# VectorE's order in the first six steps of layer 0, and where TensorE transposes the words of tiles 3 and 4

## The chip, the cores and the metric
The kernel runs on one core of a Trainium2 chip. The metric is the device time of one execution in microseconds, the median of the runs made. Everything is set down against one profiled execution, whose own time is given below.

## The reference
Two graph attention layers over N = 8192 nodes with 256 features and a dense adjacency matrix of int32 that is nearly empty:

```python
# layer 0
h = relu(layernorm(x)); Wh = h @ W
e = (Wh @ a[:256])[:, None] + (Wh @ a[256:])[None, :]
e = where(adj == 0, -1e9, e)
x = x + leaky_relu(softmax(e, axis=1) @ Wh, 0.2)
# layer 1
h = relu(layernorm(x))
e = leaky_relu((h @ a[:256]) + (h @ a[256:]).T, 0.01)
e = where(adj > 0, e, -9e15)
x = x + softmax(e, axis=1) @ h
```

In layer 0 the row's own score cancels in the softmax, so a row of the result is a masked sum of weighted rows of `Wh`, divided by the masked sum of the weights.

## The kernel before
The rows are cut into T = 64 tiles of 128. A prologue normalises x, projects it (`transpose_h`, `project`) and makes `V0`, the weighted rows of `Wh` in two fp16 parts. Then layer 0 goes over the tiles, and layer 1 follows; the change lies in layer 0's first steps.

What happens to tile t of layer 0, engine by engine:

- **SyncE** (`whole`) loads the tile's 4 MB of adjacency in four quarters (`load`; a quarter waits for the conversion of the same quarter one tile earlier), and stores the packed words, the new x and the new h (`store_words`, `store_x1`, `store_h`), all in one queue in a written order.
- **ScalarE** (`step`) converts the quarters to fp8 (`convert`, tile t + 3 in step t), copies the transposed words from PSUM (`copy_words`, tile t + 1), scales the sums of tile t - 1 (`copy_sums`, which makes `ysb`), and takes the root and the relu of layer 1's layernorm for tile t - 1 (`roots1`, `finish`).
- **VectorE** (`step`) folds the fp8 masks into words in four parts (`fold`, tile t + 2; part 0 waits for the four conversions of that tile), finds the positions of the row's edges (`make_keys`, `extract`, and `decode`, whose long part `decode_bits` runs in steps 2, 6, 10 and so on, and whose short part `decode_list` runs in every step from 2), makes the reciprocal for tile t - 1 (`normalise`), adds x (`add_x`, which waits for `ysb`), and expands the copied words of tile t + 1 into the masks `adjT` in eight instructions (`unpack`, which waits for `copy_words`).
- **TensorE** runs `aggregate` for tile t: 128 matmuls (64 row blocks `jb`, two parts) of `adjT` and `V0` into a bank. It waits first for the masks of this tile (`adjT_ready`) and for `ysb` of tile t - 2, whose bank it overwrites. Behind the matmuls of `jb == turn_at` it puts `turn` of tile t + 1, four transposes of folded words, which wait for `fold` part 3 of that tile. The default of `turn_at` is 4. Tile 1 has it at 48; tiles from 2 on run in a loop, two tiles a round.

Two tiles' worth of `adjT`, banks and words alternate. Every engine works its instructions in program order; step t of VectorE and ScalarE begins when tile t - 1 is summed, and so stands beside TensorE's sums of tile t.

Of the kernel before, what the change touches and what calls it, by code (L numbers as in the profile page):

```python
# [30 lines left out]
def two_layer_graph_attention(nc, x, adj, w0, a0, a1, key_pos, ident, tri, caps, row_ids, out):  # L31
# [32 lines left out]
    T = N // P  # L64
# [17 lines left out]
    XB = 4  # L82
    LAG = 5
    XL = 1
    UN = 4
    VU = 16
    NPK = 4
# [3 lines left out]
    NS = T - SP0  # L91
    assert NS % UN == 0 and UN == NX == NPK
    KW = 16
# [10 lines left out]
    SORT = NS + 2  # L104
# [29 lines left out]
    with outer:  # L134
# [13 lines left out]
        with ctx:  # L148
            def sb(name, shape, dt):
                return ctx.enter_context(nc.sbuf_tensor(name, shape, dt))  # L150

            def sem(name):
# [43 lines left out]
            kraw = tail[:, 0:NK]  # L196
            khi = tail[:, NK:NK + UN * KT].rearrange("p (u s) -> p u s", u=UN)
            ki = tail[:, NK + UN * KT:NK + 2 * UN * KT].rearrange("p (u s) -> p u s", u=UN).bitcast(i32)
            ktop = sb("ktop", [P, UN, KT], f32)
            kb = sb("kb", [P, UN, KT], f32)  # L200
            kone = kraw.bitcast(f16)[:, 0:UN * ROUNDS * KT]\
                .rearrange("p (u s) -> p u s", u=UN)
# [107 lines left out]
            def offset(t):  # L310
                return SPARSE if t < NS else DENSE

            @block.sync
            def _(sp):
# [43 lines left out]
                def store_x1(t, off, b):  # L358
                    sp.wait_ge(x1_ready, t + 1)
                    sp.dma_start(x1_d[bass.ds(t + off, 1), :, :].rearrange("o p n -> p (o n)"),  # L360
                                 x1[:, b, :]).then_inc(x1_out[b], 16)
# [5 lines left out]
                def whole(t):  # L367
# [7 lines left out]
                    if LAG <= t:  # L375
                        store_x1(t - LAG, offset(t - LAG), (t - LAG) % NX)
                    if XL <= t < T + XL:
                        load_x(t - XL, offset(t - XL), (t - XL) % NX, t - XL < NX)
                    if LAG + 1 <= t:
# [3 lines left out]

                for t in range(T + XL):
                    whole(t)
                for i in range(3):
                    sp.wait_ge(scattered[i], 16 * len(range(i, NS, 3)))
                sp.dma_start(rec[:, :, :], rec_d.rearrange("(m p) c -> p m c", p=P)).then_inc(rec_in, 16)
                for t in range(T + XL, T + LAG):
                    whole(t)  # L390
# [183 lines left out]
            def _(dve):  # L574
# [109 lines left out]
                with dve.Fori(0, T // VU) as k:  # L684
                    for j in range(VU):
                        t = k * VU + j
# [5 lines left out]
                def normalise(t, b):  # L692

                    dve.wait_ge(acc_ready, t + 1)
                    nc.vector.reciprocal(rden[:, b:b + 1], acc[b][:, D:DV]).then_inc(rden_ready, 1)  # L695
# [140 lines left out]
                        decode_end(e)  # L836

                def step(t, j, n_in, x1_reuse, kept, off, ahead=True, folds=True, listed=False,
                         taken=False, e=None):

                    normalise(t - 1, (j - 1) % 2)
                    if folds:
                        fold(t + 2, j % 2, 0)
                    if taken:
                        extract(t + 1, (j + 1) % UN)
                    add_x(t - 1, (j - 1) % NX, n_in, x1_reuse, kept, off)
                    if ahead:
                        unpack(t + 1, (j + 1) % 2, (j + 1) % NPK)
                    if folds:
                        fold(t + 2, j % 2, 1)  # L850
                        fold(t + 2, j % 2, 2)
                    scale_h(t - 1)
                    if folds:
                        fold(t + 2, j % 2, 3)
                    if e is not None:
                        decode(e, (j + 2) % UN)
                    if listed:
                        make_keys(t + 2, j % 2)
                    dots(t - 1, (j - 1) % NX, kept)
# [62 lines left out]
                dve.wait_ge(hh_ones, 1)  # L922
                for t in range(1, T):
                    step(t, t % UN, *counts(t), ahead=t + 1 < T, folds=t + 2 < T, listed=t + 2 < NS,
                         taken=t + 1 < NS, e=(t - 2) // UN if 2 <= t < NS + 2 else None)
                    if t == SORT:
                        sort_totals()
                    if t == SORT + 1:
                        sort_scan()
                    if t == SORT + 2:  # L930
                        sort_ranks()
# [6 lines left out]
            @block.tensor  # L938
            def _(pe):
                pe.wait_ge(w_in, 16 * 3)  # L940
                pe.wait_ge(ucol_ready, 2)

                def transpose_h(t):
                    pe.wait_ge(h_ready, t + 1)
                    if t >= 2:
                        pe.wait_ge(hT_ready, t - 1)
                    for c in range(2):
                        last = nc.tensor.transpose(tps[t % 2][:, c * P:(c + 1) * P],
                                                   H[:, t, c * P:(c + 1) * P], idf[:, :])
                    last.then_inc(tr_ready, 1)  # L950

                def project(t):
                    pe.wait_ge(hT_ready, t + 1)
                    if t >= 3:
                        pe.wait_ge(wh_ready, t - 2)
                    for c in range(2):
                        last = nc.tensor.matmul(wps[t % 3][:, 0:DV], hT[:, t % 2, c, :], w_sb[:, c, :],  # L957
                                                start=(c == 0), stop=(c == 1))
                    last.then_inc(proj_ready, 1)

                def turn(t, b, reuse=True):

                    pe.wait_ge(fold_ready, t * 3 + 3)
                    if reuse:
                        pe.wait_ge(pk_ready, t - 1)
                    pe.sem_inc(words_due, 1)
                    words = fold1[:, b, 1, :].bitcast(bf16)
                    for q in range(BQ):
                        last = nc.tensor.transpose(turned[b].bitcast(bf16)[:, q * P:(q + 1) * P],  # L969
                                                   words[:, q * P:(q + 1) * P], idb[:, :])  # L970
                    last.then_inc(words_ps, 1)

                def aggregate(t, b, v0_wait=False, reuse=True, turn_at=T // 16):

                    pe.wait_ge(adjT_ready, t + 1)
                    if reuse:
                        pe.wait_ge(ysb_ready, t - 1)
                    pe.sem_inc(masks_due, 1)
                    for jb in range(T):
                        if v0_wait:  # L980
                            pe.wait_ge(v0_ready, jb + 1)
                        for s in range(2):
                            q, i, h = place(jb)
                            last = nc.tensor.matmul(acc[b][:, 0:DV], adjT_h[:, b, i, q, :, h],  # L984
                                                    V0[:, jb, s, 0:DV], start=(jb == 0 and s == 0),
                                                    stop=(jb == T - 1 and s == 1))
                        if jb == turn_at:
                            turn(t + 1, 1 - b)
                    last.then_inc(acc_ready, 1)

                for t in range(T):
                    transpose_h(t)
                    if t >= 1:
                        project(t - 1)
                    if t == T - 14:
                        pe.wait_ge(idb_ready, 1)
                        turn(0, 0, False)
                project(T - 1)
                turn(1, 1, False)
                pe.wait_ge(wh_ready, T)  # L1000
                pe.wait_ge(ones_set, 2)
                aggregate(0, 0, v0_wait=True, reuse=False, turn_at=None)
                aggregate(1, 1, reuse=False, turn_at=3 * T // 4)
                with pe.Fori(1, SORT // 2) as k:
                    for b in range(2):
                        aggregate(k * 2 + b, b)
                for b in range(2):
                    aggregate(SORT + b, b)
                pe.wait_ge(const_in, 16 * 5)
                pe.wait_ge(totals_ready, 1)  # L1010
                nc.tensor.matmul(kps[0][:, 0:KC], trib[:, 0:P], sums2[:, 1, :], start=True, stop=False)
                nc.tensor.matmul(kps[0][:, 0:KC], trib[:, P:2 * P], sums2[:, 0, :], start=False, stop=True)\
                    .then_inc(rank_ps, 1)
                with pe.Fori(SORT // 2 + 1, T // 2 - 1) as k:
                    for b in range(2):
                        aggregate(k * 2 + b, b)
                aggregate(T - 2, 0)
                aggregate(T - 1, 1, turn_at=None)
# [667 lines left out]
```

## Time and profile before

| | us |
|---|---|
| median of 3 runs | 1916.56 (1912.78 to 1921.1) |
| profiled execution, its own time | 1914.35 |
| its span on the core | 1912.5 |
| TensorE busy, of the span | 1691.5 |
| VectorE busy | 1203.0 |
| ScalarE busy | 973.4 |
| GpSimd busy | 651.6 |

The profile is one execution. Layer 0's sums run on TensorE from about 105 to about 1058 us, layer 1 from there to the end. An average over the whole span hides where an engine waits; it is read from the timeline of the stretch. In the rows further down, a line such as `[8.78 <-DVE adjT L658]` says that the engine sat idle for 8.78 us before the first instruction of the row, and that the instruction of line 658 on VectorE (DVE) ended the wait. L984 are the matmuls of layer 0, L969 the transposes of words, L627 to L641 the four parts of `fold`, L655 and L658 `unpack`, L695 `normalise`, L492 `copy_words`, L532 `copy_sums`, L519 `roots1`.

### The profile page before, as it was taken

What the parts mean: (1) busy time and instruction counts of PE and PEld (TensorE: products, weight loads), DVE (VectorE), ACT (ScalarE), POOL (GpSimd) and SP (SyncE); (2) the same over time, 40 slices, a digit from 0 to 9 for tenths busy, and PEclk for the clock granted to TensorE, in tenths of its full rate; (3) what the DMA queues carried; (4) which work ended last, traced back from release to release, by engine and by line L of the source; (5) the groups of instructions that cost most, each with busy time, mean ns of one, the idle gap of its engine ahead of it and who ended that gap; (6) DMA issues with size and microseconds to landing.
All of it is one profiled execution on the core that took longest, in us unless ns stands there. A gap on an engine that the chain in (4) does not pass through costs nothing. (4 is left out here: it accounts for less than half of the span.)

```text
span 1912.5 us, 37724 instructions
## 1 busy us (share of the span) xinstructions
PE 1691.5 (88%) x13955; PEld 1391.3 (73%) x13955; DVE 1203.0 (63%) x4595; ACT 973.4 (51%) x1367; POOL 651.6 (34%) x607
## 2 busy tenths in 40 slices
PE   6888999999999999999999397677888888978878
PEld 5646888888888888888888285454666667757657
DVE  7488888988888888674444377652435445435434
ACT  5987665665666556666662375432333233323322
POOL 0000000000000000026665548755656657665562
PEclk9998999999999999999999698877889889979889
DMA  8529998888988889989994534533333333433331
GB/s 287 182 76 386 342 349 325 314 311 321 354 320 326 318 310 331 355 333 378 386 379 104 130 94 134 160 80 88 101 89 83 111 89 94 117 100 99 88 92 52
DMA packets 142801, 410.60 MB, mean 215 GB/s; under 512 B 26193, under 2 KB 90066, under 8 KB 109906
## 3 DMA queue, kind: packets, MB, share of 16 engines
q1 hardware_dynamic: 108434, 329.85, 47.6%
q0 software_dynamic: 27904, 73.43, 13.9%
q10 hardware_dynamic: 6336, 5.77, 1.0%
q8 instruction: 62, 1.02, 0.2%
q14 instruction: 65, 0.53, 0.1%
HBM read 368.94 MB, written 40.03 MB: 214 GB/s over the span
## 5 line engine op out<-in xcount | busy, mean ns | idle before, releaser
L984 PE MATMUL banks<-HV,adjT 128*128 128x257 f16 x8192 | 938.8, 274 | 16.7 <-DVE adjT L658 8.8
L984 PEld LDWEIGHTS banks<-HV,adjT 128*128 128x128 fp8e4 x8192 | 792.5, 98 | 148.2 <-DVE HV L688 23.7
L1639 PE MATMUL banks<-Vp,adjp 128*128 128x257 f16 x2560 | 540.6, 292 | 115.4 <-issue 59.2
L1639 PE MATMUL banks<-Vn,adjn 128*128 128x257 f16 x2560 | 538.1, 291 | 48.9 <-issue 47.7
L1264 POOL DMA_INDIRECT gat<-h_of_layer,rec x420 | 465.8, 1109 | 275.5 <-issue 117.9
L444 ACT ACTIVATE adj_f<-adj_i 128x2048 fp8e4<-128x2048 int32 x256 | 480.1, 1898 | 6.6 <-DMA adj_i<-in_adj 6.5
L1300 ACT ACTIVATE adjn<-h1bc,nh 128x512 fp8e5<-128x512 f32 x320 | 212.1, 716 | 446.2 <-remote 272.1
L1639 PEld LDWEIGHTS banks<-Vp,adjp 128*128 128x128 fp8e4 x2560 | 261.2, 103 | 192.3 <-issue 126.5
L1639 PEld LDWEIGHTS banks<-Vn,adjn 128*128 128x128 fp8e4 x2560 | 262.2, 103 | 124.8 <-issue 76.5
L425 POOL DMA_DIRECT2D HV<-x_after_layer x44 | 25.5, 580 | 773.4 <-DVE rank L911 741.3
L1473 DVE TENSOR_TENSOR adjn<-adjp,adjn 128x1024 uint16<-128x1024 uint16 x80 | 55.4, 692 | 334.8 <-ACT adjn L1300 296.0
L1534 DVE SCALAR_TENSOR_TENSOR sacc<-gat,w,sacc 128x257 f32<-128x257 f32 x332 | 152.5, 477 | 0.0
L492 ACT ACTIVATE pk<-banks 128x512 uint16<-128x512 uint16 x64 | 37.9, 593 | 170.3 <-PE banks L969 143.9
L695 DVE RECIPROCAL rden<-banks 128x1 f32<-128x1 f32 x64 | 10.7, 168 | 145.9 <-PE banks L984 115.3
L655 DVE TENSOR_SCALAR adjT<-pk 128x512 uint16<-128x512 uint16 x448 | 94.6, 282 | 0.0
L957 PE MATMUL banks<-w_sb,hT 128*128 128x257 f32 x256 | 68.9, 392 | 15.6 <-ACT hT L456 15.3
L627 DVE SCALAR_TENSOR_TENSOR fold<-adj_f 128x1024 int32<-128x1024 int32 x64 | 77.2, 1206 | 7.4 <-ACT adj_f L444 7.4
L418 POOL DMA_INDIRECT x_after_layer_sorted<-HV,rank x44 | 66.5, 1512 | 13.4 <-issue 12.2
L525 ACT ACTIVATE hh<-x,nmr,rstd 128x256 f32<-128x256 f32 x64 | 38.4, 601 | 53.6 <-DVE nmr L727 45.8
L1515 DVE TENSOR_TENSOR w<-e 128x5 f32<-128x5 f32 (+2 forms) x88 | 13.9, 157 | 77.8 <-ACT e L1321 58.5
L519 ACT ACTIVATE std<-mv,eps 128x1 f32<-128x1 f32 x64 | 18.8, 294 | 86.0 <-DVE mv L719 83.9
L1255 POOL DMA_INDIRECT out<-sout,rec x44 | 46.5, 1058 | 43.1 <-DVE sout L1550 31.8
(158 smaller groups left out, 1395.2 us busy)
## 6 DMA issues: line engine op xcount, KB each, us to landing
adj_i<-in_adj SPq DMA_DIRECT2D x256, 1024.0 KB
h_of_layer<-hh SPq DMA_DIRECT2D x64, 129.0 KB
hs<-h_of_layer SPq DMA_DIRECT2D x64, 129.0 KB
xt<-in_x SPq DMA_DIRECT2D x64, 128.0 KB
packed_adj<-pk SPq DMA_DIRECT2D x64, 128.0 KB
x_after_layer<-x SPq DMA_DIRECT2D x64, 128.0 KB
HV<-in_x SPq DMA_DIRECT2D x14, 512.0 KB, 8.8
gat<-h_of_layer,rec POOLq DMA_INDIRECT x420
```

The source lines that it names most:

```text
L418: pool.indirect_dma_start(x1s_d, bass.IndirectOffsetOnAxis(ap=rank[:, m:m + 1], axis=0), HV[:, T + m % SH, 0:D], None).then_inc(xs_out[m % ...
L444: nc.scalar.activation(adj_f[:, b, q * QC:(q + 1) * QC], adj_i[:, q, :], ACT.Copy, scale=2.0, saturate=False).then_inc(conv_done, 1)
L627: nc.vector.scalar_tensor_tensor(four, whole[:, 0:4 * GW], 1, whole[:, 4 * GW:8 * GW], ALU.logical_shift_right, ALU.bitwise_or)\
L655: last = nc.vector.tensor_scalar(adjT[:, b, i, :], pk[:, pb, :], PAIR << i, 6 - i, ALU.bitwise_and, ALU.logical_shift_left)
L957: last = nc.tensor.matmul(wps[t % 3][:, 0:DV], hT[:, t % 2, c, :], w_sb[:, c, :], start=(c == 0), stop=(c == 1))
L984: last = nc.tensor.matmul(acc[b][:, 0:DV], adjT_h[:, b, i, q, :, h], V0[:, jb, s, 0:DV], start=(jb == 0 and s == 0), stop=(jb == T - 1 and ...
L1255: pool.indirect_dma_start(out, bass.IndirectOffsetOnAxis(ap=rec[:, m, OWN:OWN + 1], axis=0), sout[:, m % NOUT, :], None).then_inc(so_out[m ...
L1264: pool.indirect_dma_start(gat[:, k % NBUF, s - s0, :], None, h_d, bass.IndirectOffsetOnAxis(ap=rec[:, m, s:s + 1], axis=0))\
L1300: i = nc.scalar.activation(adjn_b[:, c % 2, jb // 2, :, jb % 2], h1bc[:, g2, :], ACT.Relu, scale=-BIG, bias=nh2[:, tiles[j]:tiles[j] + 1], ...
L1473: nc.vector.tensor_tensor(part, both, part, ALU.bitwise_and).then_inc(neg_ready, 1)
L1534: nc.vector.scalar_tensor_tensor(acc, x, w, acc, ALU.mult, ALU.add)\
L1639: mm = nc.tensor.matmul(bank[2 * i + part][:, 0:DV], m[:, i * P:(i + 1) * P], V[:, j, s, 0:DV], start=(j == 0 and s == 0), stop=(j == T - ...
```

## The change
On VectorE, steps 1 to 6 (`hurry`, t < HURRY = 7) get another order: behind `normalise` come `unpack` of tile t + 1, then `extract` of tile t + 1, then part 0 of `fold` of tile t + 2, then `add_x`. Before, it was `fold` part 0, `extract`, `add_x`, `unpack`. The other instructions of the step keep their places, and steps from 7 on are as they were.

On TensorE, tiles 2 and 3 are taken out of the loop and written out. The transposes of tile 3's words stand behind row block 48 of tile 2's sums, those of tile 4's words behind row block 32 of tile 3's sums; before, both stood behind row block 4. The loop begins at tile 4. No instruction is added or removed on VectorE.

```diff
+    HURRY = 7
                 def step(t, j, n_in, x1_reuse, kept, off, ahead=True, folds=True, listed=False,
-                         taken=False, e=None):
+                         taken=False, e=None, hurry=False):
 
                     normalise(t - 1, (j - 1) % 2)
-                    if folds:
+                    if hurry:
+                        unpack(t + 1, (j + 1) % 2, (j + 1) % NPK)
+                        extract(t + 1, (j + 1) % UN)
                         fold(t + 2, j % 2, 0)
-                    if taken:
+                    elif folds:
+                        fold(t + 2, j % 2, 0)
+                    if taken and not hurry:
                         extract(t + 1, (j + 1) % UN)
                     add_x(t - 1, (j - 1) % NX, n_in, x1_reuse, kept, off)
-                    if ahead:
+                    if ahead and not hurry:
                         unpack(t + 1, (j + 1) % 2, (j + 1) % NPK)
                     if folds:
                         fold(t + 2, j % 2, 1)
...
-                         taken=t + 1 < NS, e=(t - 2) // UN if 2 <= t < NS + 2 else None)
+                         taken=t + 1 < NS, e=(t - 2) // UN if 2 <= t < NS + 2 else None, hurry=t < HURRY)
...
                 aggregate(0, 0, v0_wait=True, reuse=False, turn_at=None)
                 aggregate(1, 1, reuse=False, turn_at=3 * T // 4)
-                with pe.Fori(1, SORT // 2) as k:
+                aggregate(2, 0, turn_at=3 * T // 4)
+                aggregate(3, 1, turn_at=T // 2)
+                with pe.Fori(2, SORT // 2) as k:
                     for b in range(2):
                         aggregate(k * 2 + b, b)
```

## Rows read from the trace of the kernel before

**Rows 1.** Busy time by stretch: PE, PEld, DVE, ACT, POOL, clock, DMA share, GB/s.
```profile
100.00:150.00 50.00, 39.86 (x260) 21.28 (x260) 40.24 (x117) 42.54 (x75) 0.32 (x1) 0.93 0.33 126
...
300.00:400.00 100.00, 100.00 (x911) 87.39 (x910) 86.94 (x401) 65.31 (x59) 0.00 (x0) 1.00 0.92 334
...
900.00:1000.00 100.00, 100.00 (x911) 87.38 (x910) 47.12 (x181) 63.39 (x56) 67.64 (x62) 1.00 1.01 383
```

**Rows 2.** Timeline of TensorE, 95 to 175: start, length, engine, line, count, idle before.
```profile
105.32 5.17 PE L984 MATMUL banks<-HV,adjT 128*128 128x257 f16 x26 [6.02 <-DVE HV L688]
...
143.29 0.38 PE L969 MATMUL banks<-idb,fold 128*128 128x128 bf16 x4
143.51 3.51 PE L984 MATMUL banks<-HV,adjT 128*128 128x257 f16 x30
155.81 2.31 PE L984 MATMUL banks<-HV,adjT 128*128 128x257 f16 x10 [8.78 <-DVE adjT L658]
...
173.66 0.38 PE L969 MATMUL banks<-idb,fold 128*128 128x128 bf16 x4
```

**Rows 3.** Timeline of TensorE, 150 to 330.
```profile
188.18 0.38 PE L969 MATMUL banks<-idb,fold 128*128 128x128 bf16 x4
188.41 14.47 PE L984 MATMUL banks<-HV,adjT 128*128 128x257 f16 x128
...
246.29 0.38 PE L969 MATMUL banks<-idb,fold 128*128 128x128 bf16 x4
```

**Rows 4.** Timeline of VectorE, 95 to 250: steps 1 to 3.
```profile
148.77 1.22 DVE L627 SCALAR_TENSOR_TENSOR fold<-adj_f 128x1024 int32<-128x1024 int32 x1 [6.67 <-ACT adj_f L444]
...
153.89 1.47 DVE L655 TENSOR_SCALAR adjT<-pk 128x512 uint16<-128x512 uint16 x7
155.28 0.28 DVE L658 TENSOR_SCALAR adjT<-pk 128x512 uint16<-128x512 uint16 x1
...
160.04 1.23 DVE L627 SCALAR_TENSOR_TENSOR fold<-adj_f 128x1024 int32<-128x1024 int32 x1 [0.70 <-ACT adj_f L444]
...
165.35 1.47 DVE L655 TENSOR_SCALAR adjT<-pk 128x512 uint16<-128x512 uint16 x7
...
179.06 0.17 DVE L695 RECIPROCAL rden<-banks 128x1 f32<-128x1 f32 x1
179.14 1.21 DVE L627 SCALAR_TENSOR_TENSOR fold<-adj_f 128x1024 int32<-128x1024 int32 x1
...
184.43 1.47 DVE L655 TENSOR_SCALAR adjT<-pk 128x512 uint16<-128x512 uint16 x7
...
186.02 0.68 DVE L632 SCALAR_TENSOR_TENSOR fold<-fold 128x512 int32<-128x512 int32 x1
...
187.29 0.42 DVE L641 SCALAR_TENSOR_TENSOR fold<-fold 128x256 int32<-128x256 int32 x1
```

**Rows 5.** Timeline of ScalarE, 95 to 190 and 190 to 262.
```profile
143.71 0.60 ACT L492 ACTIVATE pk<-banks 128x512 uint16<-128x512 uint16 x1 [0.29 <-PE banks L969]
...
151.35 0.46 ACT L532 ACTIVATE ysb<-banks,rden 128x256 f32<-128x256 f32 x1
...
196.13 0.29 ACT L519 ACTIVATE std<-mv,eps 128x1 f32<-128x1 f32 x1 [1.88 <-DVE mv L719]
...
203.13 0.60 ACT L492 ACTIVATE pk<-banks 128x512 uint16<-128x512 uint16 x1
```

**Rows 6.** Busy time by stretch, columns as in rows 1, around the first gap.
```profile
148.00:152.00 4.00, 0.00 (x0) 0.00 (x0) 3.15 (x12) 3.01 (x3) 0.00 (x0) 0.77 1.03 421
152.00:156.00 4.00, 0.19 (x2) 0.16 (x3) 3.85 (x16) 3.57 (x4) 0.00 (x0) 0.50 1.02 430
...
160.00:162.00 2.00, 2.00 (x18) 1.64 (x16) 1.92 (x5) 1.78 (x2) 0.00 (x0) 0.89 1.00 399
```

**Rows 7.** Timeline of VectorE, 186 to 232 and 232 to 262: steps 6, 7.
```profile
216.39 0.17 DVE L695 RECIPROCAL rden<-banks 128x1 f32<-128x1 f32 x1 [2.12 <-PE banks L984]
...
235.47 0.17 DVE L695 RECIPROCAL rden<-banks 128x1 f32<-128x1 f32 x1
...
243.69 0.42 DVE L641 SCALAR_TENSOR_TENSOR fold<-fold 128x256 int32<-128x256 int32 x1
...
247.04 0.17 DVE L695 RECIPROCAL rden<-banks 128x1 f32<-128x1 f32 x1
```

## The prediction, made before the changed kernel had run
> **What bounds the kernel now.** I read the busy times by stretch first, to see which engine sets the pace of layer 0. From 300 to 400 us TensorE is busy for all 100 us, and from 900 to 1000 us again, while VectorE has 87 and 47 us of work in them [rows 1]. So from some early point TensorE runs without a gap until its sums end, and whatever moves that point moves everything behind it, one for one. From 100 to 150 us it is busy for 40 of 50 us: there the time can change.
>
> Next came TensorE's timeline, for the gaps. Between the sums of tile 1 (last 30 matmuls from 143.51 to 147.02) and those of tile 2 (from 155.81) it idles 8.78 us and is released by VectorE's masks, `adjT` [rows 2]. Behind it, the transposes of the words mark the tiles: they stand at 173.66 (tile 4), 188.18 (tile 5) and 246.29 (tile 9), and 246.29 minus 188.18 is four times 14.53, so a tile takes 14.53 us and nothing stalls after tile 2 [rows 2, 3].
>
> Then VectorE's timeline, for why the masks were late. It sits idle for 6.67 us until 148.77, for the conversions that `fold` of tile 3 needs, then extracts, adds x of tile 0, and unpacks tile 2 only from 153.89 to 155.56 [rows 4]. The words of tile 2 had been copied by 144.31 [rows 5]. The reader is to see two things: the masks could have been made in that idle time; and from 148.77 on VectorE itself has hardly a gap for three steps (step 2 has its fold at 160.04 and is over by 179.06, the unpacking of tile 4 runs from 184.43 to 186.1, and the fold of tile 5 ends at 187.71) [rows 4]. TensorE began tile 4 at 188.18 less 1.13 us for ten matmuls, 187.05, and asked for the fold of tile 5 at 188.18 [rows 3]. VectorE was ready only 1.0 and 0.5 us ahead. In these steps a delay of VectorE is soon one of TensorE.
>
> **The change, part by part.** The sum goes against the profiled execution, 1914.35 us (span 1912.5); the median of the runs is 1916.56.
>
> Step 1, order on VectorE. Unpacking tile 2 starts at 144.35 and takes 1.67 us, so it ends at 146.0. TensorE is free at 147.02, but it also waits for `ysb` of tile 0, for the bank that tile 2's sums overwrite. ScalarE makes that from 151.35 to 151.81, behind conversions that wait for their data [rows 5]; nothing in the change touches those. With the 0.25 us that lay between the last mask and the first matmul [rows 2, 4], tile 2 starts at 152.06: 3.75 us earlier. The wait has changed its owner and lost less than half. The extraction fits into the rest of the idle time; `fold` of tile 3 still starts at 148.77; x is added from 151.85 instead of 152.42. The fold's last part, behind the square root, ends near 156.8 against 157.2, and the step's dots stay where they were, behind the same conversions. So step 2 begins at 159.2 as before.
>
> The clock. At 148 to 152 us the granted share is 0.77, at 152 to 156 it is 0.50, the lower of the two levels (1.2 GHz), and at 160 to 162 it is 0.89 [rows 6]. TensorE had been idle since 147.02. A share of 0.77 in four microseconds means that the fall was near 150.2, before my 152.06. So tile 2 starts slow again: before, it took from 155.81 to 173.66 less 1.13, that is 172.53, or 16.72 us instead of 14.53 [rows 2, 3]. The price is 2.19 us, and I keep it. Tile 2 ends at 168.78.
>
> The later transpose of tile 3. It stands behind matmul pair 48 of 63, with 30 matmuls left (3.40 us) and 0.22 us of its own, so it starts at 165.16 and ends at 165.54; the copy on ScalarE is done at 166.18. The old place, pair 4, would have come near 154 us, ahead of the fold at 156.8, and cost TensorE 2.5 us or more; this is saved. But now VectorE's step 2 begins with a wait for these words: from 159.2 to 166.18 it does nothing, and extraction, fold, x, decoding and dots queue behind it. On ScalarE the conversions stand behind `copy_words` of tile 3 as well, and on SyncE the loads behind `store_words`; I price that at 0, since the queues move 0.92 of their time in the steady part and TensorE waits for none of it there [rows 1]; if this cover fails, it is the slower rival below. Unpacking tile 3 ends at 167.85, in time for 168.78. Tile 3's sums then run to 183.31. Tile 4's transpose, at pair 32, comes at 176.3, and its fold is there at 174.8: no stall.
>
> Step 2, the rest. From the fold to the unpacking was 165.35 minus 160.04, 5.31 us; the unpacking took 1.59 until the next instruction (184.43 to 186.02), which puts its end in step 2 at 166.94, and from there to 179.06 was 12.12 us, the first long decoding among it [rows 4]. New: 166.18 + 1.59 + 5.31 + 12.12 = 185.20, 6.1 us later than before. Now unpacking tile 4 comes first, from 185.28 to 186.95, and TensorE starts tile 4 at 187.20. Before it was 187.05. The 3.75 us are gone, and TensorE has idled 3.9 us ahead of tile 4.
>
> Step 3. TensorE wants the fold of tile 5 after ten matmuls. That fold stands behind extraction, fold and x (5.29 us, 179.14 to 184.43) and 1.69 us more (to the end of 187.29's, from 186.02) [rows 4]: 186.87 + 5.29 + 1.69 = 193.85, and 0.2 for the semaphore gives 194.05. Before: 188.18. That is 5.87 us later. TensorE idles about 5 us here, and after it the clock is taken as low, for 2.19 us once more; 0 if the ten matmuls and the shorter gaps keep it up. The running loss is 8.06 us.
>
> On the clock, the Trainium skill ("TensorE: Matmul & The Clock Gate", What's actually happening) has the lower level as the default, released by activity and lost when idle. The trace agrees in the gap before tile 2 [rows 6]; by the rule both new gaps lead to the low level, which is the 2.19 us already counted.
>
> Steps 4 to 6. Here unpacking moves ahead of its words: the transpose comes ten matmuls into the sums, and ScalarE's copy comes after its conversions. From the root to the copy's end ScalarE took 203.13 + 0.60 minus 196.13, 7.6 us, of which 0.75 were a wait that goes [rows 5]: 6.85. With x of tile 2 at 192.1, words 5 come at 199.1. From one set of words to the next, while VectorE waits for them, are then 1.59 + 5.25 + 0.1 + 6.85, 13.8 us. A step with a list decoded is 11.57 us (235.47 to 247.04) [rows 7], so step 5 starts at 199.1 + 11.57 = 210.7 and words 6 come at 212.9; step 6 starts at 224.5 and words 7 come at 226.7. Step 6 holds the long decoding: 235.47 minus 216.39 is 19.08 [rows 7], so step 7 starts at 245.8. There, in the old order, masks 8 are done at 252.8 (5.39 + 1.67) and the fold of tile 9 at 245.8 + 8.64 = 254.4 [rows 7]. TensorE, 8.06 late, ends tile 7 at 253.2 and asks for that fold at 254.36; it gets it at 254.6. Against 246.29 this is 8.3 us. If the clock cost nothing in step 3, TensorE would arrive 2.2 us earlier here and wait for the same VectorE instructions: 8.3 again. After step 7 the order is the old one, VectorE catches up by step 9, and nothing is recovered, as TensorE has no gap to give back.
>
> The two sums taken out of TensorE's loop: tile 1's sums are written out as well and ran at 3.51 us for 30 matmuls, the loop's at 14.47 for 128 [rows 2, 3], 0.117 and 0.113 us each. I take 0; from the difference it could be 1 us for 256, and on the other side nothing speaks for a gain.
>
> The sum: -3.75 from the first gap, +3.90 given back in step 2, +5.72 in step 3 (5.87 less the 0.15 already counted), +2.19 clock, +0.24 at tile 9: 8.3 us. Forecast 1916.56 + 8.3 = 1924.9 (1922.7 for a profiled execution). Bounds: no clock price, with steps 4 to 6 quick enough to leave no wait at tile 9, gives +5.9; another low-clock start at tile 9 and 1 us of straight code give +11.5.
>
> **The rivals.**
> Gain kept: the masks' wait is shorter and later steps absorb the delay. The time is then 1916.56 - 3.75 = 1912.8. For it: the gap is real and the early masks remove their part. Against: VectorE had 1.0 and 0.5 us in hand and is set back 6.1. Chance 12%.
>
> Small loss: VectorE's rows in steps 2 and 3 shrink, because the fold and the extraction no longer wait for anything, and half of the 5.87 goes: about +3, 1919.6. Against: the rows show no waits in them. Chance 10%.
>
> Slower beyond the forecast: step 6, where words 7 arrive and the 19.08 us step starts. Each microsecond by which they are later than 226.7 comes back as a wait for masks 8 and fold 9; from 1.3 us on the total passes +9.6, and with 2 us and a low clock behind it, it is 8.3 + 2 + 2.19 = 12.5, 1929.1. For it: ScalarE's copy stands behind four conversions whose data must have landed, on a DMA that I took to have room. Chance 16%.
>
> **How the numbers follow.** Forecast 62%, own range 1921 to 1929. The bound of 0.5%, about what a measurement of this kernel can tell from no change, is 9.6 us. The forecast lies 1.3 us under it, and runs of one kernel spread by some 4 us either way, so a third of it falls beyond: 21% slower, 41% same. The small loss is same (10%), the slower rival slower (15 and 1), the kept gain same 8, faster 4. Together slower 0.36, same 0.60, faster 0.04. The range, 1915 to 1931, leaves out the kept gain and the worst of the slower rival.
>
> **What would show it.** Right: TensorE's first gap ends at 152, released by ScalarE's `ysb`; VectorE idles about 7 us before unpacking tile 3; gaps on TensorE of about 4 us before tile 4, released by `adjT`, and of about 5 us ten matmuls later, released by `fold`; waits of VectorE for ScalarE's words in steps 4 to 6. Wrong: masks 4 done before 183.3, or tile 5's transposes before 189; then the gain stands. Wrong too if TensorE shows gaps inside the written-out sums.

## The result and the profile after

| | us |
|---|---|
| the changed kernel, first measurement | 1947.42 (1935.75 to 1950.49, 5 runs) |
| the kernel before beside it | 1917.0 (1912.78 to 1928.01, 5 runs) |
| ratio | 1.0137, 95% interval 1.0092 to 1.0183 |
| profiled execution of the changed kernel | 1935.75, span 1933.7 |
| changed kernel again, 12 runs against 29 | 1760.79 against 1754.18, ratio 1.0032 (1.0015 to 1.0049) |
| changed kernel a third time, 12 runs against 23 | 1918.05 against 1913.08, ratio 1.0038 (1.0003 to 1.0073) |

The change makes the kernel slower: all three intervals lie above 1. The forecast was +8.3 us, in a range up to 1931, and the first median lay 16 us above the range. The two later measurements give 0.0032 x 1754 = 5.6 us (2.6 to 8.6 by the interval) and 0.0038 x 1913 = 7.3 us (0.6 to 14). All ratios here and below are those on record, taken from undisturbed runs alone, and need not equal the quotient of two medians of all runs. The text takes the two parts in turn: layer 0, which the prediction worked out and the traces confirm, and layer 1, which the change does not touch and whose time moved by 11.9 us between the first two traces.

TensorE's timeline of the changed kernel, to be read beside [rows 2, 3]. The matmuls of layer 0 are now L989, the transposes of words L974:

```profile
144.12 0.38 PE L974 MATMUL banks<-idb,fold 128*128 128x128 bf16 x4
144.34 3.52 PE L989 MATMUL banks<-HV,adjT 128*128 128x257 f16 x30
152.86 13.71 PE L989 MATMUL banks<-HV,adjT 128*128 128x257 f16 x98 [5.00 <-issue]
166.42 0.38 PE L974 MATMUL banks<-idb,fold 128*128 128x128 bf16 x4
...
177.37 0.38 PE L974 MATMUL banks<-idb,fold 128*128 128x128 bf16 x4
177.59 7.09 PE L989 MATMUL banks<-HV,adjT 128*128 128x257 f16 x62
188.51 1.85 PE L989 MATMUL banks<-HV,adjT 128*128 128x257 f16 x10 [3.83 <-DVE adjT L659]
195.29 0.58 PE L974 MATMUL banks<-idb,fold 128*128 128x128 bf16 x4 [4.92 <-DVE fold L642]
195.67 16.21 PE L989 MATMUL banks<-HV,adjT 128*128 128x257 f16 x128
211.72 0.38 PE L974 MATMUL banks<-idb,fold 128*128 128x128 bf16 x4
...
255.62 0.38 PE L974 MATMUL banks<-idb,fold 128*128 128x128 bf16 x4 [0.16 <-DVE fold L642]
```

The wait of 5.00 us is put down to "issue" here; what came last is seen on ScalarE, where `ysb` is done at 152.77, and TensorE starts at 152.86:

```profile
152.31 0.46 ACT L533 ACTIVATE ysb<-banks,rden 128x256 f32<-128x256 f32 x1
```

The words of tile 2 are turned (transposed) at 144.12 here and at 143.29 before; this 0.83 us comes from the prologue, and is taken off every time below that is compared. The one gap of 8.78 us has become three: 5.00, 3.83 and 4.92. The last transposes shown, those of tile 9, stand at 254.79 against 246.29: 8.5 us late, where 8.3 was forecast. The sums end as late:

```profile
1031.00 27.66 PE L984 MATMUL banks<-HV,adjT 128*128 128x257 f16 x246
```
```profile
1040.32 27.66 PE L989 MATMUL banks<-HV,adjT 128*128 128x257 f16 x246
```

The first row is of the kernel before (the sums end at 1058.66), the second of the changed one (1067.98, or 1067.15 without the prologue's part). So layer 0 is 8.5 us longer. Layer 1 took 1912.5 - 1058.66 = 853.8 us before and 1933.7 - 1067.98 = 865.7 after: 11.9 of the 21.2 us between the two spans lie where no instruction was changed. The medians are 30.4 us apart; the other 9 us lie between the profiled executions and the medians, and no trace shows in which layer.

VectorE's timeline of the changed kernel shows who made TensorE wait, to be read beside [rows 4]:

```profile
145.17 1.51 DVE L656 TENSOR_SCALAR adjT<-pk 128x512 uint16<-128x512 uint16 x7 [2.25 <-ACT pk L493]
...
152.79 0.43 DVE L707 SCALAR_TENSOR_TENSOR lr<-ysb 128x256 f32<-128x256 f32 x1 [1.96 <-ACT ysb L533]
...
167.47 1.50 DVE L656 TENSOR_SCALAR adjT<-pk 128x512 uint16<-128x512 uint16 x7 [7.14 <-ACT pk L493]
...
186.49 0.17 DVE L696 RECIPROCAL rden<-banks 128x1 f32<-128x1 f32 x1
186.58 1.48 DVE L656 TENSOR_SCALAR adjT<-pk 128x512 uint16<-128x512 uint16 x7
...
194.72 0.42 DVE L642 SCALAR_TENSOR_TENSOR fold<-fold 128x256 int32<-128x256 int32 x1
```

The masks of tile 2 are made from 145.17, while VectorE would have been idle. But the masks of tile 3 wait 7.14 us for their words, and all the work behind them, the decoding of step 2 among it, moves. The masks of tile 4 start at 186.58, and TensorE has stood idle for them since 184.68. The fold of tile 5 ends at 195.14 and TensorE turns its words at 195.29.

Busy time by stretch, columns as in [rows 1], for the clock, beside [rows 6]:

```profile
152.00:156.00 4.00, 3.14 (x15) 2.25 (x16) 2.33 (x6) 3.36 (x4) 0.00 (x0) 0.50 1.04 435
...
183.00:188.00 5.00, 1.68 (x16) 1.22 (x13) 4.72 (x27) 1.31 (x2) 0.00 (x0) 1.00 0.76 252
188.00:190.00 2.00, 1.49 (x10) 1.12 (x10) 1.91 (x12) 0.97 (x1) 0.00 (x0) 0.76 0.06 16
190.00:192.00 2.00, 0.36 (x2) 0.00 (x0) 1.96 (x5) 0.00 (x0) 0.00 (x0) 0.50 0.94 311
192.00:196.00 4.00, 0.71 (x6) 0.67 (x7) 3.65 (x19) 2.40 (x3) 0.00 (x0) 0.50 0.58 199
```

Tile 2 starts at the lower level (0.50, 1.2 GHz), as forecast. In the gap ahead of tile 4 the clock is still full and falls only once the sums have begun again (0.76 from 188 to 190, where they begin at 188.51); it stays low through the third gap and into the sums behind it, and is full again from 200 us on.

### The profile page after: what moved, and what is told of

Its sections match the earlier page's. It is cut to its first block and busy times, and to the rows that moved or that the text cites. A ratio compares the mean times of both kernels' runs of the same rounds, so it can differ in the third digit from the quotient of the medians.

```text
span 1933.7 us, 37717 instructions
## 1 busy us (share of the span) xinstructions
PE 1691.4 (87%) x13955; PEld 1390.9 (72%) x13955; DVE 1204.3 (62%) x4595; ACT 972.2 (50%) x1367; POOL 648.6 (34%) x607
## 5 line engine op out<-in xcount | busy, mean ns | idle before, releaser
L989 PE MATMUL banks<-HV,adjT 128*128 128x257 f16 x8192 | 941.9, 274 | 16.7 <-DVE HV L689 7.5
L989 PEld LDWEIGHTS banks<-HV,adjT 128*128 128x128 fp8e4 x8192 | 794.1, 98 | 149.7 <-DVE HV L689 23.3
L1328 ACT ACTIVATE e<-gat,hb 128x5 f32<-128x5 f32 (+3 forms) x176 | 41.5, 288 | 40.0 <-DMA gat<-h_of_layer,rec 40.0
```

What stands on the lines that cost most here:

```text
L1328: nc.scalar.activation(e8[:, k % 2, i, 0:s1 - s0], gat[:, k % NBUF, 0:s1 - s0, DV], ACT.Exp, scale=scale, bias=hb[:, i, m:m + 1]).then_inc ...
```

## The experiments

In what follows a theory is named by the letter that it has in the expectations. Layer 0 of each run is compared in the trace, with the start of tile 2's word transposes as the common origin. Their prologues end up to 1.8 us later than that of the kernel before.

**Is it the longer program on TensorE?** The loss in layer 1 was the surprise, so the first question was whether layer 1's code, moved by the sums that are written out, runs worse. The tiles written out alone:

```diff
-                with pe.Fori(1, SORT // 2) as k:
+                aggregate(2, 0)
+                aggregate(3, 1)
+                with pe.Fori(2, SORT // 2) as k:
```

> The kernel before, with the sums of tiles 2 and 3 written out ahead of TensorE's loop, their transposes still behind row block 4, and VectorE as before. It adds no work and changes no order; it only makes TensorE's program longer ahead of everything that follows. Theory A (the part of the loss that lies in layer 1 comes from where TensorE's later code lies): layer 0 ends at the same time as before within 1 us, layer 1 is 12 to 25 us longer, about 1930 to 1940. Rival B (layer 1 loses because layer 0 ends later, or by chance): both layers as before, 1912 to 1925.

Measured: 1920.99 (10 runs) against 1919.56 (31 runs), ratio 1.0039 (0.9998 to 1.008). Its layer 0 ends at 1058.85 against 1058.66, and its transposes up to tile 10 stand within 0.2 us of before; its layer 1 took 842.7 us. Theory A wanted at least 12 us more in layer 1 and got 11 less in the trace. The interval leaves room for up to 15 us more, not for the 26 us of the first ratio.

The other test of the same theory moves layer 1's code by another distance, in an idle stretch:

```diff
                 nc.tensor.transpose(bank[7][0:T, 0:P], h1all[:, :], idf[:, :]).then_inc(h1T_ps, 1)
+                for _ in range(128):
+                    pe.sem_inc(pad, 1)
```

> The kernel before with 128 increments of an unused semaphore on TensorE at the start of layer 1, behind its first transpose, where TensorE sits idle for 15 us before its first masks. They do nothing but move the code of layer 1 by 128 instructions. Layer 0 is untouched. Theory A (code place matters): layer 1 changes by several us, either way. Rival B: no change, 1912 to 1925.

Measured: 1919.34, ratio 1.0014 (0.9975 to 1.0053), layer 1 in its trace 857.3 us. With up to 10 us inside the interval, this run alone does not close the question. Theory A falls as the cause of 12 to 25 us in layer 1 when the changed kernel itself is measured again below, at 1.0032 and 1.0038. One of the ten runs took 1950.81 us: such a long execution happens with layer 0 as before, too.

**The order on VectorE alone**, with TensorE's program as before; against the changed kernel:

```diff
-                aggregate(2, 0, turn_at=3 * T // 4)
-                aggregate(3, 1, turn_at=T // 2)
-                with pe.Fori(2, SORT // 2) as k:
+                with pe.Fori(1, SORT // 2) as k:
```

> VectorE's new order in steps 1 to 6 alone; TensorE's program as before, the words of tiles 3 and 4 turned behind row block 4. By the working of the prediction: tile 2's sums start at 152, then TensorE waits 2.5 to 3 us for the fold of tile 3; unpacking tile 3 starts near 162.6, step 3 near 181.7, masks 4 are ready near 183.6 and TensorE does not wait for them, the fold of tile 5 comes near 190.6 against 188.2; with one more slow start layer 0 ends 2.5 to 5 us later. Theory A (code place): layer 1 as before, in all 1919 to 1923. Rival B (layer 1 answers to a late layer 0): layer 1 loses some 10 us too, 1930 or more.

Measured: 1916.97, ratio 0.9987 (0.9943 to 1.0031). TensorE's timeline (tile 2's words at 143.94):

```profile
152.69 2.31 PE L989 MATMUL banks<-HV,adjT 128*128 128x257 f16 x10 [5.02 <-ACT ysb L533]
157.62 0.59 PE L974 MATMUL banks<-idb,fold 128*128 128x128 bf16 x4 [2.62 <-DVE fold L642]
...
191.26 0.38 PE L974 MATMUL banks<-idb,fold 128*128 128x128 bf16 x4 [2.63 <-DVE fold L642]
```

The row of tile 2 names the new owner of the first wait, ScalarE's `ysb`; in the changed kernel the same wait is put down to "issue". Less 0.65 for the origin, tile 2 starts at 152.04 (forecast 152.06), waits 2.62 us for the fold of tile 3, does not wait for masks 4, and turns tile 5's words at 190.61 (expected 190.6). Layer 0 ends 4.6 us later than before. So even alone the new order loses in layer 0: what it puts ahead of the folds makes the transposes wait. The time of the whole kernel cannot tell 4.6 us from none here. Its upper bound, 1.0031, does rule out the other theory, B, that layer 1 answers to a late layer 0 with 10 us of its own.

**TensorE's part alone**, the changed kernel with the new order in no step:

```diff
-    HURRY = 7
+    HURRY = 0
```

> TensorE's part alone: tiles 2 and 3 written out, transposes behind row blocks 48 and 32, VectorE in the old order throughout. Tile 2 starts at 155.8 as before; the words of tile 3 are turned near 168.9 and VectorE waits for them from 165.4 to 169.9; masks 4 come near 190.7 where TensorE is free at 187.1, and tile 5's transposes near 192.5 against 188.2: layer 0 ends 4.3 us later, 6.5 with a slow start. Theory A: layer 1 is 12 to 25 us longer, as with the tiles written out alone, in all 1933 to 1948. Rival B: 1921 to 1935.

Measured: 1923.2, ratio 1.0005 (0.9957 to 1.0053). Layer 0 ends 8.9 us later, not 4.3 to 6.5, and VectorE shows why:

```profile
171.96 0.43 DVE L707 SCALAR_TENSOR_TENSOR lr<-ysb 128x256 f32<-128x256 f32 x1 [6.89 <-ACT ysb L533]
```

I had let VectorE wait at the unpacking, from 165.4. But in the old order `add_x` stands ahead of it, and wants `ysb`, which ScalarE makes only behind `copy_words`. So VectorE stops 1.65 us of work earlier than I had it, and masks 3 end near 174.1 and not 171.5: `copy_words`, waiting for late words, holds `ysb` behind it on ScalarE as well. The two parts of the change lose 4.6 and 8.9 us alone and 8.5 together. The losses don't add: with the words of tile 3 at block 48 the loss is nearly the same in either order. That is because both are times in which VectorE's queue stands or is behind, as I read it; no run separates them further.

**Only the place of tile 3's words.** The changed kernel with them behind block 24:

```diff
-                aggregate(2, 0, turn_at=3 * T // 4)
-                aggregate(3, 1, turn_at=T // 2)
+                aggregate(2, 0, turn_at=24)
+                aggregate(3, 1)
```

> The changed kernel with the words of tile 3 turned behind row block 24 of tile 2's sums and not 48, and those of tile 4 behind 4 and not 32. ScalarE can copy the words of tile 3 only after two conversions, near 162.6, so block 24 costs it nothing, while block 48 kept VectorE waiting until 166.2. If the late words of tile 3 are what gave the gain back: VectorE unpacks tile 3 at 162.6, masks 4 are ready near 183.4, about when TensorE ends tile 3 (183.3), so the gap ahead of tile 4 shrinks from 3.8 us to under 1; the wait for the fold of tile 5 stays, 5 to 6 us, as unpacking and extraction still stand ahead of it; layer 0 ends 4 to 5 us later than before and not 9. Rival (the decoding of step 2 alone decides): the gap ahead of tile 4 stays near 4 us.

Measured: 1758.42 against 1754.18, ratio 1.0029 (1.0008 to 1.0049). TensorE's timeline, tile 2's words at 145.09:

```profile
153.76 7.18 PE L989 MATMUL banks<-HV,adjT 128*128 128x257 f16 x50 [4.94 <-issue]
...
174.08 0.59 PE L974 MATMUL banks<-idb,fold 128*128 128x128 bf16 x4 [3.08 <-DVE fold L642]
174.46 15.82 PE L989 MATMUL banks<-HV,adjT 128*128 128x257 f16 x128
193.17 0.38 PE L974 MATMUL banks<-idb,fold 128*128 128x128 bf16 x4 [2.90 <-DVE fold L642]
```

The gap ahead of tile 4 is gone, as the theory wanted, and layer 0 ends 1065.86 - 1.80 - 1058.66 = 5.4 us later instead of 8.5. I had missed that tile 4's words, back at block 4, now come ahead of their fold, 3.08 us. The wait for the fold of tile 5 was 2.90 us and not 5 to 6, since TensorE came to it later. Taking away one wait of the chain exposes the next: every one of these meetings has to be moved with the others.

**A version meant to keep the gain**: the new order in steps 1 and 3 only, and each transposition late enough for its fold and early enough for ScalarE.

```diff
-    HURRY = 7
+    HURRY = (1, 3)
...
-                         hurry=t < HURRY)
+                         hurry=t in HURRY)
...
-                aggregate(2, 0, turn_at=3 * T // 4)
-                aggregate(3, 1, turn_at=T // 2)
-                with pe.Fori(2, SORT // 2) as k:
+                aggregate(2, 0, turn_at=24)
+                aggregate(3, 1)
+                aggregate(4, 0, turn_at=24)
+                aggregate(5, 1, turn_at=8)
+                with pe.Fori(3, SORT // 2) as k:
```

> A version meant to keep the gain: the new order on VectorE in steps 1 and 3 only, where its words are there already, and the words of tiles 3, 4, 5 and 6 turned behind row blocks 24, 4, 24 and 8, so that no transposes come before their fold and no words later than ScalarE could copy them before. By the rows of the kernel before: tile 2 starts at 152.06, 3.75 us earlier, VectorE's steps keep their times, masks 4 are ready near 180.8, the fold of tile 5 at 187.7 is asked for near 188.9, masks 5 are ready at 197.7 for 197.8. Layer 0 ends 3 to 4 us earlier than before with no gap behind the first. Rival: one of these meetings is missed and half or all of it is given back, 0 to 2 us earlier. In all 1912 to 1917 against 1917 to 1920 of the kernel before; within its noise.

Measured: 1753.46 against 1754.18, ratio 0.9988 (0.997 to 1.0007). TensorE's timeline, tile 2's words at 144.23:

```profile
152.77 7.05 PE L989 MATMUL banks<-HV,adjT 128*128 128x257 f16 x50 [4.81 <-issue]
...
169.22 1.27 PE L989 MATMUL banks<-HV,adjT 128*128 128x257 f16 x10 [0.47 <-DVE adjT L659]
...
170.82 0.38 PE L974 MATMUL banks<-idb,fold 128*128 128x128 bf16 x4 [0.33 <-DVE fold L642]
...
199.90 2.17 PE L989 MATMUL banks<-HV,adjT 128*128 128x257 f16 x18 [0.89 <-DVE adjT L659]
```

Tile 2 starts 4.0 us earlier than before, and three small waits are left, of VectorE. Layer 0 ends at 1056.95 - 0.94 = 1056.01, 2.65 us earlier than before: seven tenths of the 3.75 that I had worked out. Of the whole time this is 0.15%, inside the interval: it is seen in the trace of layer 0, and the whole time can't show it. It is the one version of the new order tried whose layer 0 is not behind that of the kernel before.

**The changed kernel again, twice.**

> The changed kernel once more, with more runs of it and of the kernel before. Layer 0 ended 9.3 us later in its first trace; the medians differed by 30 us, the rest of it in layer 1, whose program is unchanged. Theory C (layer 1 takes a time that differs from run to run by some 15 us either way, and five runs of each gave an unlucky pair of medians): the ratio comes down to about 1.005, +9 us. Rival D (layer 1 answers to the change): the ratio stays at 1.010 or above, +20 us or more.

Measured: the ratio 1.0032 of the table above, layer 0's gaps 4.47, 3.84 and 5.04 us, and a surprise: the kernel before took 163 us less than in the first measurement, and the changed one 187. In its trace layer 0 ends at 1067.39, 8.1 us later than before, and layer 1 takes 693.3 us where it took 853.8 and 865.7. Executions thus come in two kinds, a long one (some 1915 us) and a short one (some 1755). The change was still to be measured again in the long kind:

> The changed kernel once more. Two kinds of executions have been seen: layer 1 takes 842 to 868 us in one set of traces and 690 to 698 in another, and in the first TensorE sits idle over 100 us in layer 1 in pieces that no engine's work ends. The changed kernel has been measured often in the second kind only, at 1.0032. Theory C (the 30 us of the first medians were mostly layer 1's own scatter): if this run is of the first kind, the ratio is 1.003 to 1.008, far under the 1.0137 first seen; in the second kind 1.003 again. Rival D (the change makes layer 1 slower where TensorE has these idle pieces): 1.010 or more in the first kind.

Measured: 1.0038, in executions of the long kind (layer 1 in the trace 851.7 us), with layer 0 7.0 us later than before. The effect of the change is 0.3 to 0.4% in both kinds, as theory C had it, and rival D falls. Theory C's account of the first pair, a bad draw from one scatter, is not shown by this; see the end of the next section.

The short set and this one were run on the same chip, so the kind does not go with the chip.

**What makes layer 1 longer in one kind.** TensorE's waits in the changed kernel over the whole span (who waited for what, us in total, times, longest), first in the long kind:

```profile
PE banks L1646 <- issue: 123.9, 175, 15.6
PE banks L1646 <- DVE x1g L1504: 21.1, 4, 9.1
```

and in the short one:

```profile
PE banks L1646 <- DVE Vn L1445: 42.5, 9, 15.9
PE banks L1646 <- DVE x1g L1504: 22.6, 4, 9.4
```

"Issue" is idle time that nothing in the profile ends. In the long kind there are 124 us of it on TensorE in layer 1; in the short kind no such row. The granted clock is lower too. Layer 1 as one stretch, the long kind first, with columns as in [rows 1]:

```profile
1065.83:1917.50 851.67, 667.61 (x5121) 515.46 (x5121) 410.59 (x1193) 308.42 (x651) 513.69 (x465) 0.86 0.37 101
1067.39:1760.70 693.31, 594.02 (x5122) 504.85 (x5121) 414.67 (x1193) 307.93 (x651) 517.33 (x465) 0.94 0.45 124
```

Of the 158 us between them, 74 are busy time of TensorE, with the clock at 0.86 against 0.94, and 85 are idle time. The idle pieces also fall between matmuls where the program has no wait. In the trace of the kernel before, these are the two matmuls of one pair (`s` = 0 and 1, same masks, same bank):

```profile
1090.62 0.27 PE L1639 MATMUL banks<-Vp,adjp 128*128 128x257 f16 x1 [1.84 <-issue]
1092.71 0.38 PE L1639 MATMUL banks<-Vp,adjp 128*128 128x257 f16 x1 [1.82 <-issue]
```

So no semaphore explains these. One guess was that TensorE waits for its own instructions:

```diff
-                def group(g, first):
-                    for c in range(NC):
...
+                def group(g, first):
+                    block(g, first, 0, True)
+                    with pe.Fori(1, 3) as k:
+                        block(g, first, k, False)
+                    block(g, first, 3, False)
```

> The kernel before with layer 1's sums on TensorE written as an inner loop of 4 chunks in place of 16 chunks in line; the middle two of four passes read the weighted rows of the first 16 row blocks and not their own, so part of the sum is another one, with the same number and shape of matmuls, waits and signals. The program that TensorE steps through in a group of tiles falls from 1024 matmuls to 768, of which 256 are passed twice. Theory C2 (the idle pieces in layer 1 that nothing ends are TensorE waiting for its own instructions, since the group's program is longer than what is held near the engine): in the first kind of execution the idle time ended by nothing falls from 111 to 153 us to under 40 and layer 1 takes 700 to 780 us; in the second kind no change, within 5 us. Rival D2 (they come from something else, such as the clock or the transfers): layer 1 stays as it is in both kinds.

Measured in the long kind, against the same 1913.08: 1914.16, ratio 1.0023 (0.9986 to 1.0059), and its layer 1 took 836.8 us. Of the two queues of kind "instruction", q8 moved less than half, and q14 as much as before (0.53 MB):

```profile
q8 instruction: 62, 1.02, 0.2%
```
```profile
q8 instruction: 28, 0.46, 0.1%
```
```profile
PE banks L1642 <- issue: 116.1, 175, 3.5
PE banks L1642 <- issue: 63.3, 109, 1.1
```

The first row (packets, MB, share) is of the kernel before, the others of this one: 0.46 MB for 1.02, and 116 us of idle time in 175 pieces, where the kernel before had 107 in 163. The last row is the stretch from 1430 to 1880 us alone. In it q8 carried no packet at all and q14 ten (0.08 MB), and still 63 us of the idle time lie there. Theory C2 falls. What stops TensorE in the long kind stays open.

## Why the prediction was right in layer 0 and wrong in the time

**The first gap** was right. The masks of tile 2 come early and `ysb` ends the wait: tile 2 starts at 152.03, forecast 152.06, a gain of 3.8 us. The slow start behind it came as well, 13.56 us from there to the words of tile 3 (152.86 to 166.42) where 13.10 were forecast.

**The gain given back in step 2** was right. Tile 3's words were turned at 165.59 (forecast 165.16), VectorE unpacked them from 166.64 (166.18), step 3 began at 185.66 (185.20), and TensorE started tile 4 at 187.68 (187.20).

**The fold of tile 5** was right: its words at 194.46, forecast 194.05.

**The clock behind it.** From those transposes to the next are 211.72 - 195.29 = 16.43 us, against 14.53 between two warm ones: 1.90 us for a forecast of 2.19. The clock was at 0.50 from 190 to 196 us and at 1.00 from 200 to 204, one low spell behind both gaps. The Trainium skill's rule ("TensorE: Matmul & The Clock Gate", What's actually happening) held: the lower level came with idleness and went with activity.

**Steps 4 to 6** were right. VectorE waited 2.05, 2.06 and 1.53 us for words in them, step 7 began at 246.81 - 0.83 = 245.98 (245.8), and the fold of tile 9 was late by 0.16 us. Words 7 were unpacked from 227.79 - 0.83 = 226.96, 0.3 us behind the forecast; the rival "slower beyond the forecast" wanted 1.3. The written-out sums cost nothing: no idle time inside them.

**The sum of layer 0**, term by term, forecast and measured: first gap -3.75 and -3.78; given back in step 2, 3.90 and 4.41; step 3, 5.72 and 5.65; clock 2.19 and 1.90; at tile 9, 0.24 and 0.32. That is 8.3 and 8.5 us. The rivals "gain kept" and "small loss" are wrong here. The closeness is in part luck: in the two later traces layer 0 was 8.1 and 7.0 us longer, and in the last of them tile 2 began at 151.31.

**The step that failed** is the size of the scatter, in "How the numbers follow": "runs of one kernel spread by some 4 us either way", and with it the sum, in which layer 1 had no term. The 4 us were read from three runs. Thirty-one runs of the kernel before went from 1902.71 to 1934.36, and layer 1 alone took 837 to 868 us in the eight traces of the long kind (843 to 859 in those of the kernel before, the written-out tiles, the order alone and the moved code). A median of five against a median of five can be 10 us off with this, by my estimate from those thirty-one, and the range had no term for it. I took layer 1 for a constant, because the change does not touch it, and looked at none of its rows.

The traces put the difference into idle time. TensorE's idle time in layer 1 that nothing ends was 106.8 us in the kernel before and 130.5 in the first trace of the changed one, while its busy time there was 673.3 and 669.5. The mechanism in layer 0 held, and with 12 runs each the forecast of 8.3 us lies inside both intervals, 5.6 (2.6 to 8.6) and 7.3 (0.6 to 14).

**What stays open.** The five first runs of the changed kernel lay from 1935.75 to 1950.49, the twelve of the third measurement, of the same kind, from 1911.92 to 1936.89, and only one of the twelve lies above the lowest of the five. So the scatter within one set does not explain the first median: the failed step accounts for some 10 of the 22 us between forecast and measured difference, not for all. That the first set met other conditions than the runs of before beside it is the reading left, and no run shows it.

## What to carry to other kernels

Before work is moved ahead of a wait, list for each engine in the loop what it will wait for next, and when each of those meetings would come: here one gap of 8.8 us became three of 13.8 in all, because the late words held VectorE for 7.1 us, and VectorE had only 1.0 and 0.5 us in hand. A hand-over between engines has a window, from the time its input is ready to the time its taker is free anyway; putting it later than the window moves the wait to the taker and to everything in its queue. And look at the scatter of the parts of a kernel that the change leaves alone before a range is given: compare a local change by its own stage in the trace.

## What the runs showed that was not expected

The same program took 1754 us in one set of runs and 1913 to 1920 in others. In the changed kernel's three traces layer 0 ended within 2.2 us of the same time; the difference is layer 1. Over all traces that took 690 to 698 us in the short kind and 837 to 868 in the long one, with 107 to 144 us of unexplained idle time on TensorE and a lower mean clock. Neither the place of the code nor the length of the loop body moved it beyond the scatter.

In the changed kernel's first trace the clock stayed full through a gap of 3.83 us and fell after it, when ten matmuls were on their way. In the trace of the third measurement it was down to 0.50 by 185 us, inside the same gap of 3.82 us (to 185.73), and the tile behind the third gap then took 2.85 us more than a warm one (192.50 to 209.88) and not 1.90. So the price of a gap can come behind it, and differs between executions of one program.
